# A routed first feed-forward network in a three-stage kernel: only the two chosen experts are computed, in blocks of 256 places

## The reference

```
def ffn(x):                                     # x: normalised tokens
    w = softmax(x @ router_w + router_b)        # 8 experts
    top, which = top_k(w, 2)
    mask = zeros.at[which].set(top / sum(top))  # 6 of 8 entries are zero
    h1 = gelu(einsum('btd,nde->btne', x, W1) + b1)      # all 8 experts
    out = einsum('btne,nef->btnf', h1, W2) + b2         # 256 -> 128 -> 256
    return sum(out * mask[..., None], axis=-2)

x = x + 0.5 * ffn(layernorm(x))
x = x + attention(layernorm(x))   # windows of 64 tokens with both neighbours, 8 heads,
                                  # plus a full attention over 256 tokens chosen by rank
x = x + 0.5 * ffn(layernorm(x))
```

## Time and profile before

| | us |
|---|---|
| median of 3 runs | 2146.27 (2138.19 to 2148.26) |
| the profiled execution | 2135.63 |
| its span | 2133.8 |
| busy: PE / DVE / ACT / POOL | 2024.4 / 1583.7 / 1243.3 / 1037.2 |
| granted clock of PE, mean | 0.99 of full speed |

### The profile page before, as it was taken

How to read it: one execution, slowest core, us unless ns; L and a number is a source line. 1 busy time by engine, 2 the same in 40 slices (tenths; PEclk the granted TensorE clock), 3 DMA queues, 4 the chain that set the end, 5 groups by cost and what they waited for, 6 DMA issues and landing times.

```text
span 2133.8 us, 40198 instructions
## 1 busy us (share of the span) xinstructions
PE 2024.4 (95%) x13232; PEld 1578.9 (74%) x13232; DVE 1583.7 (74%) x5212; ACT 1243.3 (58%) x2953; POOL 1037.2 (49%) x1150
## 2 busy tenths in 40 slices
PE   7999999989999999999998998998999899999998
PEld 6888888876766666666666665766667688888887
DVE  6988888988676676677576576675765488888887
ACT  5555555656656657657657557567556555555554
POOL 4444445545536447347247246256254444444444
PEclk9999999999999999999999999999999999999999
DMA  6111111000011011011011011011013111111110
GB/s 235 58 60 41 41 41 41 30 21 18 33 40 41 16 54 32 11 60 36 1 65 31 1 65 31 1 65 31 3 52 121 37 40 36 36 39 40 35 36 31
DMA packets 72326, 91.19 MB, mean 43 GB/s; under 512 B 6432, under 2 KB 66232, under 8 KB 71096
## 3 DMA queue, kind: packets, MB, share of 16 engines
q1 hardware_dynamic: 61368, 69.39, 9.5%
q0 software_dynamic: 8448, 18.95, 3.1%
q10 hardware_dynamic: 2304, 0.28, 0.1%
HBM read 40.23 MB, written 48.37 MB: 42 GB/s over the span
## 4 chain that ended last, share of the span: by engine, by line
PE 56%; DVE 21%; issue 9%; POOL 9%; ACT 4%; DMA 0%; DVEq 0%; POOLq 0%; ACTq 0%
PE bank L530 10%; PE bank L532 9%; PE bank L531 9%; PE bank L749 5%; PE bank L738 5%; PE bank L709 4%; PE bank L720 4%; PE bank L681 3%; DVE st L1043 3%; PE bank L557 3%; DVE xb L1133 2%; POOL hl L1373 2%; POOL tri L1348 2%; DVE wt L1104 2%; ACT prob L967 1%
## 5 line engine op out<-in xcount | busy, mean ns | idle before, releaser
L1421 POOL TENSOR_TENSOR prob<-prob,rden 128x512 f32<-128x512 f32 x320 | 335.6, 1050 | 539.4 <-DVE rden L1273 537.3
L1133 DVE SCALAR_TENSOR_TENSOR xb<-bank,gate,xb 128x256 f32<-128x256 f32 x1024 | 423.5, 476 | 91.5 <-PE bank L532 89.9
L1373 POOL TENSOR_TENSOR hl<-hf,hh 128x512 fp32r<-128x512 f32 x256 | 330.2, 1296 | 221.0 <-ACT hh L837 211.9
L967 ACT ACTIVATE prob<-prob,nmax 128x256 f32<-128x256 f32 x512 | 256.2, 503 | 279.9 <-DVE nmax L1255 278.0
L836 ACT ACTIVATE hf<-bank,b1s 128x512 f32<-128x512 f32 x256 | 176.3, 689 | 335.5 <-PE bank L532 328.3
L1255 DVE CUSTOM_DVE_ANT_0 prob<-bank,mask 128x256 f32<-128x256 f32 x512 | 195.2, 418 | 142.8 <-PE bank L709 141.2
L1267 DVE COPY probT<-bank 128x512 f32<-128x512 f32 x160 | 110.3, 689 | 127.2 <-PE bank L720 127.1
L709 PE MATMUL bank<-kT,qT 64*128 64x256 f32 x1024 | 191.6, 429 | 13.7 <-ACT prob L967 9.5
L720 PE MATMUL bank<-ident,prob 128*128 128x128 f32 x1280 | 197.2, 277 | 4.4 <-POOL prob L1421 4.1
L720 PEld LDWEIGHTS bank<-ident,prob 128*128 128x128 f32 x1280 | 156.0, 142 | 58.6 <-issue 17.7
L738 PE MATMUL bank<-probT,V 128*64 128x128 f32 x2048 | 169.1, 286 | 6.2 <-ACT oT_s L983 4.8
(11 more groups left out here) (179 smaller groups left out, 5256.1 us busy)
## 6 DMA issues: line engine op xcount, KB each, us to landing
xb<-in_L_attn_x SPq DMA_DIRECT2D x16, 512.0 KB, 3.8
x_d<-xb SPq DMA_DIRECT2D x16, 512.0 KB, 2.9
x<-x_d SPq DMA_DIRECT2D x8, 1024.0 KB
x_d<-x SPq DMA_DIRECT2D x8, 1024.0 KB, 4.3
xb<-x_d SPq DMA_DIRECT2D x16, 512.0 KB, 3.8
out<-xb SPq DMA_DIRECT2D x16, 512.0 KB, 2.8
hrow<-hs_d SPq DMA_DIRECT2D x16, 257.0 KB, 2.6
w<-w_d SPq DMA_DIRECT2D x4, 1024.0 KB, 11.2
```

The costliest lines, as they stand in the source:

```text
L967: act.activation(prob[j % NP][:, h, :], src, ACT.Exp, bias=nmax[:, j % 4, h:h + 1], scale=-1.0 if light else 1.0, accum_out=den[:, j % 4, ...
L1133: dve.scalar_tensor_tensor(out=x, in0=bank[ob][:, (t % 2) * D:(t % 2 + 1) * D], scalar=gate[:, k % 2, t, e:e + 1], in1=x, op0=ALU.mult, op ...
L1373: pool.tensor_tensor(lo[:, :], f[:, :], h[:, :].bitcast(F32), ALU.subtract).then_inc(s_hl)
L1421: pool.tensor_tensor(prob[j % NP][:, :, :], prob[j % NP][:, :, :], rden[:, j % 4, :].unsqueeze(2).broadcast_to([P, 2, KEYS]), ALU.mult).th ...
```

## The change

The first FFN is written anew; the second keeps its code. The tokens are handled in three batches: rows 0 and 1, rows 2 to 4, rows 5 to 7 (4, 6 and 6 groups).

1. **Groups.** For each group: statistics, rstd, normalisation, transposes, logits, routing, power, gates. Then DVE and PE count for every token how many before it in the batch chose the same expert (`group_spots`: a triangular matrix and ones, by matmul), which gives each of its two choices a place in a tensor in DRAM (spots_d). POOL sends the normalised tokens there with 8 indirect DMAs (`send`: 4 tiles by 2 choices).
2. **Table.** Behind a batch's last group DVE makes a table (`batch_table`): for each block of 256 places its expert and its row in spots_d. An expert with n places has n/256 blocks, rounded up. The number of blocks is fixed at 23, 31 and 31 (the full ones, and 7 that the rounding can need): 85.
3. **Blocks.** In each of them SP reads the row number from the table into a register and loads 256 places (`block_load`); PE transposes them; ACT copies the expert's first weights (chosen by a register, `w1_copy`) and the high part of the input; DVE makes the low part; PE computes the hidden layer and, two ticks later, the output (`block_out`, again with a register for the weights); ACT, POOL and DVE do gelu, low part and bias. SP stores the result in order of blocks (made_d). At the start of each batch SP also fills up each expert's last block with zeros (`pads`: 8 register reads and 8 transfers).
4. **Gathering.** The attention loads its tokens from the input itself, and for each tile of 128 tokens POOL fetches the two parts from made_d with two indirect DMAs (`fetch`), which DVE adds, each times its share (`combine`). x1_d is gone.

The order is set by ticks. GROUP_AT says in which tick a group begins; its pieces follow 1 to 10 ticks later. Block s begins in tick 25 + s. Row 0's gathering, layernorms and selection scores stand in ticks 80 to 100, so the slots begin at -20 instead of -40. For rows 1 to 7 the gathers stand two in a slot from slot 40b - 45, the adds from 40b - 39, and the layernorms move by some slots.

```diff
+BATCH = ((0, 2), (2, 5), (5, 8))
+BLK = 256
+    BLOCKS = [n + E - 1 for n in LEAST]
+    STEPS = sum(BLOCKS)
...
+        STEP0 = 25
+        TICKS = STEP0 + STEPS + 5
+        GROUP_AT = (0, 4, 8, 12, 16, 20, 24, 27, 30, 34, 38, 43, 48, 53, 58, 63)
+        ROW0 = STEP0 + FIRST[2] + 1
...
-            return range(-SLOTS, SLOTS * ROWS + 16)
+            return range(-SLOTS // 2, SLOTS * ROWS + 16)
...
+        def got_slot(b, i):
+            return SLOTS * b - 45 + i // 2
+        def add_slot(b, t):
+            return SLOTS * b - 39 + t
         def stat1_slot(b, q):
-            return SLOTS * b - 38 + q // 2
+            return SLOTS * b - 38 + q
...
+            def pads(n):
+                sp.wait_ge(s_tab, NTAB * (n + 1))
+                for e in range(E):
+                    row = value(sp, pad_row[n][0:1, e:e + 1], 0, SPARE[n] - BLK)
+                    sp.dma_start(spots_d[n][bass.ds(row, BLK), :].rearrange("(p s) d -> p s d", s=BT), zeros[:, :, :]).then_inc(s_zero, 16)
+            def block_load(s_):
+                n = batch_of(s_)
+                if s_ == FIRST[n]:
+                    pads(n)
+                    sent(sp, n)
+                    sp.wait_ge(s_zero, 16 * E * (n + 1))
+                    sp.wait_ge(s_spare, 16 * (n + 1))
+                if s_ >= 4:
+                    sp.wait_ge(s_bT, s_ - 3)
+                row = value(sp, block_row[n][0:1, s_ - FIRST[n]:s_ - FIRST[n] + 1], 0, SPARE[n] + (E - 2) * BLK)
+                sp.dma_start(xin[s_ % 4][:, :, :], spots_d[n][bass.ds(row, BLK), :].rearrange("(p s) d -> p s d", s=BT)).then_inc(s_bld[s_ % 4], 16)
...
+            def block_hidden(s_):
+                pe.wait_ge(s_blo, s_ + 1)
+                pe.wait_ge(s_w1c, s_ + 1)
+                if s_ >= 2:
+                    pe.wait_ge(s_bge, s_ - 1)
+                for c in range(C):
+                    ins = mm3(bank[2 + s_ % 2][:, 0:BLK], [w1_now[s_ % 2][:, n, c, :] for n in range(2)], [x[s_ % 2][:, c, :] for x in (xh, xl)],
+                              start=(c == 0), stop=(c == C - 1))
+                ins.then_inc(s_bh)
...
+            for tau in range(TICKS):
+                todo = tick_jobs(tau)
+                for s_ in step_at(tau):
+                    block_turn(s_)
+                for what in todo[0:1]:
+                    job(*what)
+                for s_ in step_at(tau - 1):
+                    block_hidden(s_)
+                for what in todo[1:]:
+                    job(*what)
+                for s_ in step_at(tau - 3):
+                    block_out(s_)
...
+            def w1_copy(s_):
+                e_act[s_] = value(act, block_e[n][0:1, s_ - FIRST[n]:s_ - FIRST[n] + 1], 0, E - 1)
+                if s_ >= 2:
+                    act.wait_ge(s_bh, s_ - 1)
+                act.activation(w1_now[s_ % 2][:, :, :, :].rearrange("p w c f -> p (w c f)"),
+                               w1_s[:, bass.ds(e_act[s_], 1), :, :, :].rearrange("p a w c f -> p (a w c f)").bitcast(F32), ACT.Copy).then_inc(s_w1c)
...
+            def block_left(s_):
+                e = value(dve, block_e[n][0:1, s_ - FIRST[n]:s_ - FIRST[n] + 1], 0, E - 1)
+                dve.wait_ge(s_bo, s_ + 1)
+                dve.tensor_tensor(yout[s_ % 4][:, :, :], view(4 + s_ % 2, "p (t n) -> p t n", t=BT),
+                                  b2_all[:, bass.ds(e, 1), :].broadcast_to([P, BT, D]), ALU.add).then_inc(s_by)
+            def combine(b, t):
+                x = x1[b % 2][:, t, :]
+                for c, part in ((0, y_row), (1, z_row)):
+                    dve.wait_ge(s_got[2 * t + c], 16 * (b + 1))
+                    dve.scalar_tensor_tensor(out=x, in0=part[:, t, :], scalar=share[:, k, c, q:q + 1], in1=x, op0=ALU.mult, op1=ALU.add).then_inc(s_comb)
...
+            def send(k, i):
+                c, q = i % 2, i // 2
+                if i == 0:
+                    pool.wait_ge(s_pos, NPOS * (k + 1))
+                    pool.wait_ge(s_norm[0], 2 * k + 2)
+                pool.indirect_dma_start(spots_d[batch_of_group(k)], bass.IndirectOffsetOnAxis(spot[:, k, c, q:q + 1], 0), xb[k % 4][:, q, :], None).then_inc(s_sc[k % 4], 16)
+            def fetch(b, i):
+                t, c = divmod(i, 2)
+                pool.indirect_dma_start(part[:, t, :], None, made_d[n], bass.IndirectOffsetOnAxis(home[:, 2 * b + t // TG, c, t % TG:t % TG + 1], 0)).then_inc(s_got[i], 16)
...
+            for tau in range(TICKS):
+                for s_ in step_at(tau - 2):
+                    block_hl(s_)
+                for k in group_at(tau, 0):
+                    rstd(0, k, 2 * k)
+                for k in group_at(tau, 4):
+                    exp2nd_a(k)
+                for i in range(8):
+                    for k in group_at(tau, 7 + i // 2):
+                        send(k, i)
```

806 lines of the change are left out of this document (597 added, 209 removed).

## The result

| | us |
|---|---|
| median after / before | 2167.59 / 2147.06 (4 runs each) |
| ratio, 95% interval | 1.0103 [1.0076, 1.0131] |
| profiled execution, span | 2166.1 (before 2133.8) |
| first maximum of the attention | 442.1 (before 488.3, forecast 419) |
| from there to the end of the span | 1724.0 (before 1645.5) |

The forecast was 2106, and faster. The first stage ends 46 us earlier, and the rest takes 79 us longer. The spans differ by 32 us and the medians by 20.5, because the profiled execution of the kernel before is one of its shortest (2135.6 at a median of 2147.1).

A forecast was written before the change was run, and what follows sets the result against it. The prediction took PE to bound the first FFN, with POOL setting the pace after the change while it sends. 69 us gained less 28 in the attention took 2135.6 to 2095, plus 10.7 for the median: 2106, range 2030 to 2190.

The forecast's parts named there:

- Constants: Start of the kernel, before DVE's first statistics: memsets, iotas and casts, taken to last until 9 us.
- first batch: First stage, first 4 groups: POOL's period 13.8 us each, 55 in all, all sent at 83, first block turned at 89.
- last 36 ticks: End of the first stage: 17 ticks with only a block, 19 with row 0's preparation, and pad clearing; together 103 us.
- drain: Emptying of the first stage's pipeline, with two projections in it, before the first maximum: 8 us.
- bare tick: First stage, a tick with only a block: 2.3 us, 1.8 of work plus 0.5.
- Register reads: PE, ACT and DVE read the expert's number, SP the block's row, per block: taken as 0.7 us, bounds 0 and 2.6.
- rival B: POOL's paired indirect DMAs, first stage and attention, cost more than 1.01 us: 256 x 0.33 = 84, to 2190; chance 0.20.
- Step 4: First stage from 83 to 290: POOL sets the pace with 12 groups and some 49 blocks, 207 us.
- Rival D: First stage: half-idle PE drops to its lower clock, ticks become 3.9 us, 42 us more: 2148, no change; chance 0.06.
- The attention pays: Attention, rows 1 to 7: gathers on POOL and adds on DVE cost 4 us a row, 28 for seven.
- upper bound of 9: Attention, us a row if neither POOL's 7 nor DVE's 2 is hidden: 63 instead of 28, 2141; chance 0.06.
- The sum: Whole kernel: first stage ends 69 us earlier, attention pays 28, net 41; profiled 2095, median 2106.

## Why the prediction was wrong, point by point

- **Constants, first batch, last 36 ticks, drain: right in length.** The first block and the lengths of the last two steps came within 1 us. In the tail that is partly luck, as two errors cancel: a bare tick took 1.88 us, not 2.3 (ACT, start of one gelu pair to the next: 405.15 to 407.03), and the ticks with the pads and row 0's part took longer.

```profile
405.15 0.47 ACT L1144 ACTIVATE hf<-bank,b1s 128x256 f32<-128x256 f32 x1
...
407.03 0.47 ACT L1144 ACTIVATE hf<-bank,b1s 128x256 f32<-128x256 f32 x1
```

- **Register reads: below the value taken.** Chosen were 0.7 us between 0 and 2.6. The engines' queues show (ns, min/median/max):

```profile
L699 ACTq TENSOR_LOAD <-block_e x85: 272/279/1262, 78.8 to 414.7; - x85
L699 SPq TENSOR_LOAD <-block_row x85: 263/271/1039, 85.8 to 408.8; - x85
L699 PEldq TENSOR_LOAD <-block_e x85: 295/337/1147, 102.2 to 419.1; - x85
L699 DVEq TENSOR_LOAD <-block_e x85: 298/306/1172, 108.4 to 421.3; - x85
```

0.27 to 0.34 in the median, up to 1.26. The Trainium skill (DMA: Bandwidth & Descriptors, section Latency and other measured facts) has a floor of about 600 ns for such a load. Here most reads are shorter, so the measurement decides.
- **Indirect DMAs (rival B): the size was right.** 0.99 us a send and 0.95 to 1.0 a gather. Of B's mechanism, dearer DMAs in pairs, little came: 0.30 us instead of 0.16 to 0.18 ahead of one that follows another, less than the 0.16 more from which B decides. The kernel did get slower, as B said, but not by that.
- **Step 4, "POOL sets the pace" (207 us): 228, from 84.1 to 312.0.** What was missing in the sum is the ring over SP: a group load that waits for landed sends, ahead of block loads. It costs 22 us at the first maximum, all of them back in the run that moved the load, where the step takes 206 (85.4 to 291.1). Each engine's busy time was counted, and no queue behind a waiting instruction on SP. POOL was busy for 69% there and not over 80%.
- **Rival D, the clock: it fell, but no run shows that it cost step 4 anything.** The clock was 0.82 from 90 to 312, and moving one wait on SP brought the 22 us back with the clock still at 0.85. What the clock itself costs there stays open. The Trainium skill (TensorE: Matmul & The Clock Gate, Part 1) says that the array is slowed unless activity releases it. The trace agrees with that (0.82 with PE busy for 74%). In the attention the clock may be part of what the order costs.
- **"The attention pays" 4 us a row: the step that failed.** It paid 11.2, more than the upper bound of 9. The gathers' part was taken as 1.5 us a row, mostly hidden, and was 4.8. DVE's adds were taken as 2.5 and were 4.1. Both had been priced by each engine's own busy time, with DVE's adds at the 0.42 of the earlier trace rows, as if POOL's work beside them cost DVE nothing. The kernel before already showed the other price, a 128x128 operation of the same kind in the ranking (ns, min/median/max):

```profile
L1227 DVE SCALAR_TENSOR_TENSOR sjunk<-srow,scol,not_later x128: 340/1115/1407, 472.7 to 1584.2; 128x128 uint8<-128x128 f32 x128
```

Its median is more than three times its shortest. The moved order had no term at all, and cost 1.9 a row.
- **The sum.** 23 us late at the first maximum and 51 more in the attention turn a gain of 41 into a loss of 33; the spans differ by 32. The forecast of 2106 also added 10.7 us, by which the median before lies over its profiled execution. In the changed kernel that distance is nothing, so its median is 62 us over the forecast and not 74.

## What to carry to other kernels

Price an added operation on a shared in-order engine by what it does to its neighbour's operations in the slots where it stands, and not by its busy time: with the gathers in POOL's queue, DVE's first add of a tile took 1.22 us in the mean instead of 0.57. When a transfer waits for others to land, ask what is queued behind it on the issuing engine; three ticks later in the program were worth 22 us. And a low share and a low clock of an engine do not show that it is the bound: here a stage got 22 us back while both stayed nearly as they were.

## What was not expected of the hardware

- DVE's adds and casts on SBUF tiles do not run beside POOL's tensor operations: 0.47 us alone, up to 3.06 with two of those in a row, and 3.76 for a cast of 128x2 numbers beside four.
- They do run beside POOL's indirect DMAs (0.47 to 0.52 us), and an add that reads a bank runs beside both (0.41 to 0.43).
- Whether a waiting operation of DVE gets in between two POOL operations without a pause is open: the cast waited for the last of four, and a product in the kernel before (710.71, 1.03 us) got in behind the first of two.
- Behind another indirect DMA, POOL begins the next 0.30 us later; behind another operation it is 0.16 to 0.17.
- Register reads of 0.27 to 0.34 us in the median, on four engines.
